# Three taps of q moved to VectorE, the convolutions finished half by half, rank from one difference, and an earlier first low part in a one-core transformer-block kernel

## The reference

```python
x = x + conv_part(_ln_c(x))                     # normalised over the 96 channels
t = tokens(x)                                   # 2304 tokens x 96
t = t + experts(_ln_t(t))
...
# conv_part
qkv = einsum('bchw,oc->bohw', x, w_qkv) + b_qkv
qkv = qkv.reshape(b, 3*c, 24, 2, 24, 2).max(axis=(3, 5))      # 576 pixels are left
qkv = depthwise_conv_3x3(qkv, w_dw) + b_dw                     # nine taps for each channel
q, k, v = split(qkv);  q, k = q/|q|, k/|k|                     # 8 heads of 12 channels
attn = (q @ k.T) * temperature                                 # 12 x 12 in each head
out = sum of topk_softmax(attn, kk) @ v * a_kk   for kk in 6, 8, 9, 9
out = repeat(gelu(out), 2x2) @ w_proj + b_proj
...
# experts: gates from softmax, best 2 of 4, weights renormalised
h = gelu(x @ w1[e] + b1[e]);  y = h @ w2[e] + b2[e];  out = sum of gate[e] * y
```

## Time and profile before

| what | value |
|---|---|
| median of 3 runs | 160.51 us (160.54, 160.51, 158.21) |
| the profiled execution | 157.93 us, of which the span is 156.1 us |
| PE busy | 142.7 us, 91% of the span |
| VectorE (DVE) busy | 116.4 us, 75% |
| ScalarE (ACT) busy | 81.8 us, 52% |
| GpSimd (POOL) busy | 62.3 us, 40% |
| mean granted TensorE clock | 0.952 |

### The profile page before, as it was taken

One profiled execution on the slowest core, in us unless ns is written; L12 is line 12 of the kernel. 1 busy time (PEld: TensorE's weight loads), 2 busy tenths in 40 slices (PEclk: granted clock), 3 DMA queues, 4 the chain that ended last, 5 costly groups with the idle time before them and its releaser, 6 DMA issues.

```text
span 156.1 us, 2515 instructions
## 1 busy us (share of the span) xinstructions
PE 142.7 (91%) x791; PEld 119.8 (77%) x791; DVE 116.4 (75%) x314; ACT 81.8 (52%) x150; POOL 62.3 (40%) x63
## 2 busy tenths in 40 slices
PE   6948968999998897699999999999999999999990
PEld 2423947999988693697866679999999999999950
DVE  0897787999958569956910489998899889899722
ACT  3371768404063243057567763767566566666540
POOL 8999981695000000230050564342332532235250
PEclk9995699999999999569999999999999999999998
DMA  4599100000000000000000001001001001000101
GB/s 142 203 231 264 38 0 4 2 0 0 0 4 0 0 0 2 0 0 4 0 0 0 0 0 42 0 2 38 2 0 38 0 0 35 2 0 4 38 0 38
DMA packets 3750, 4.43 MB, mean 28 GB/s; under 512 B 1934, under 2 KB 3290, under 8 KB 3644
## 3 DMA queue, kind: packets, MB, share of 16 engines
q1 hardware_dynamic: 3338, 3.86, 9.7%
q10 hardware_dynamic: 402, 0.44, 0.8%
HBM read 3.42 MB, written 0.88 MB: 28 GB/s over the span
## 4 chain that ended last, share of the span: by engine, by line
PE 75%; DVE 16%; DMA 3%; ACT 3%; issue 1%; SPq 1%; DVEq 0%
PE psum L937 17%; PE psum L938 16%; PE psum L939 16%; PE psum L1105 8%; PE psum L979 3%; PE psum L975 3%; PE psum L974 3%; DMA xT<-xt 3%; PE psum L1078 3%; DVE stats L665 2%; DVE xn_lo L643 2%; PE psum L932 1%; DVE stats L717 1%; DVE xnT L720 1%; PE psum L910 1%
## 5 line engine op out<-in xcount | busy, mean ns | idle before, releaser
L437 POOL TENSOR_TENSOR xs<-xs,yg 96x384 f32<-96x384 f32 x23 | 26.4, 1147 | 45.4 <-DVE yg L872 37.3
L656 DVE TENSOR_TENSOR h_lo<-hf,h_hi 128x768 fp32r<-128x768 f32 x25 | 34.4, 1375 | 5.2 <-ACT hf L549 4.7
L937 PE MATMUL psum<-xn_hi,w_hi 97*128 97x384 f32 (+1 forms) x72 | 29.7, 413 | 2.2 <-DVE xn_lo L643 2.2
L938 PE MATMUL psum<-xn_hi,w_lo 97*128 97x384 f32 (+1 forms) x72 | 25.4, 353 | 0.0
L939 PE MATMUL psum<-xn_lo,w_hi 97*128 97x384 f32 (+1 forms) x72 | 25.3, 351 | 0.0
L549 ACT ACTIVATE hf<-psum 128x768 f32<-128x768 f32 x25 | 20.2, 809 | 5.7 <-PE psum L939 5.7
L430 POOL TENSOR_TENSOR xs<-xs,pr 96x384 f32<-96x384 f32 x6 | 5.1, 868 | 37.8 <-DVE gs L704 27.8
L937 PEld LDWEIGHTS psum<-xn_hi,w_hi 97*128 97x128 f32 x72 | 14.4, 200 | 5.3 <-issue 4.3
L937 PE MATMUL psum<-h_hi,w_hi 128*96 128x384 f32 x50 | 17.0, 340 | 0.0
L938 PE MATMUL psum<-h_hi,w_lo 128*96 128x384 f32 x50 | 16.8, 336 | 0.0
L939 PE MATMUL psum<-h_lo,w_hi 128*96 128x384 f32 x50 | 16.8, 336 | 0.0
(11 more groups left out here) (173 smaller groups left out, 284.2 us busy)
## 6 DMA issues: line engine op xcount, KB each, us to landing
xs<-x SPq DMA_DIRECT2D x1, 864.0 KB, 10.0
out<-xs SPq DMA_DIRECT2D x6, 144.0 KB, 1.9
w1s<-w SPq DMA_DIRECT2D x1, 576.0 KB
w2s<-w SPq DMA_DIRECT2D x1, 576.0 KB, 6.8
xT<-xt SPq DMA_DIRECT2D x1, 432.0 KB, 5.0
xT<-xt SPq DMA_DIRECT2D x1, 288.0 KB, 3.7
pars<-par ACTq DMA_DIRECT2D x1, 196.5 KB
cst<-consts ACTq DMA_DIRECT2D x1, 170.0 KB, 5.0
```

Of the source, the lines that this page charges most:

```text
L437: pool.tensor_tensor(cols(xs, c), cols(xs, c), cols(yg, e), ALU.add).then_inc(acc_done, 1)
L656: dve.tensor_tensor(lo, h, hi.bitcast(F32), ALU.subtract).then_inc(h_split, 1)
L937: pe.matmul(o, w_hi, m_hi, start=start, stop=False)
L938: pe.matmul(o, w_lo, m_hi, start=False, stop=False)
```

## The change

Four edits, and some that go with them.

1. Taps 0 to 2 of q leave PE. VectorE makes them into a new tile `qpart`, with the bias of q, each one ahead of the same tap of v. q's convolution on PE has taps 3 to 8. VectorE adds PE's half and `qpart` into `qkc`, in place of ScalarE's L508. Tap 8 of v stands beside the first step of k's `rnorm` chain.
2. `conv` does one half of the image to its end (high inputs, then low ones) before the other. ScalarE squares each half of k by itself.
3. The rank is made from `ahead = other - own`, compared with a constant that is 0, or just under 0 for j < i, instead of two comparisons, a product and a sum.
4. `low_from_bank(1, 0)` moves from inside the `rsqrt` of the second norm to ahead of its last two statistics.

With them, ScalarE's high part of `w2` moves ahead of q's diagonals and GpSimd's low part of `w2` ahead of k's; 3 idle products are added behind q's convolution and 2 ahead of the first product.

```diff
-IDLE = {"start": 24, "before scores": 1, "softmax": 1}
+IDLE = {"start": 24, "convolved": 3, "before scores": 1, "softmax": 1, "turned": 2}
...
+Q_TAPS = 3
+KNORM_AT = 8
...
+            pool.wait_ge(w_high, 2)
+            low(w2_lo[:, :], w2s[:, :], w2_hi[:, :], w_split)
             pool.wait_ge(kp_split, 1)
             low(kp_lo[:, :], pooled[:, PAD * PAD:2 * PAD * PAD], kp_hi[:, :], kp_split)
-            pool.wait_ge(w_high, 2)
-            low(w2_lo[:, :], w2s[:, :], w2_hi[:, :], w_split)
...
             for b in range(2):
+                half = slice(PIX + b * HP, PIX + (b + 1) * HP)
                 act.wait_ge(kconv_done, b + 1)
-                act.activation(qkc[:, PIX + b * HP:PIX + (b + 1) * HP], bank(4 + b, cols=HP), ACT.Identity,
+                act.activation(qkc[:, half], bank(4 + b, cols=HP), ACT.Identity,
                                bias=pars[0:C, P_BDW + 1:P_BDW + 2]).then_inc(k_ready, 1)
-            act.wait_ge(k_ready, 2)
-            act.activation(sqj[:, :], qkc[:, PIX:], ACT.Square, accum_out=ssq[:, 1:2]).then_inc(ssq_done, 1)
+                act.wait_ge(k_ready, b + 1)
+                act.activation(sqj[:, b * HP:(b + 1) * HP], qkc[:, half], ACT.Square,
+                               accum_out=ssq[:, 1 + 2 * b:2 + 2 * b]).then_inc(ssq_done, 1)
             act.wait_ge(knorm_done, 1)
             act.activation(khat[:, :], qkc[:, PIX:], ACT.Copy, scale=rnorm[:, 1:2]).then_inc(khat_ready, 1)
-            for b in range(2):
-                act.wait_ge(qmm_done, b + 1)
-                act.activation(qkc[:, b * HP:(b + 1) * HP], bank(b, cols=HP), ACT.Identity,
-                               bias=pars[0:C, P_BDW:P_BDW + 1]).then_inc(qconv_done, 1)
...
                 for k in range(TPC + 7, NT):
+                    if k == NT - 2:
+                        low_from_bank(1, 0)
                     statistics(k)
-                scale(slice(TPC, NT), beside_second).then_inc(ln[1]["rstd"], 1)
+                scale(slice(TPC, NT), None).then_inc(ln[1]["rstd"], 1)
...
+            def whole_tap(g, t, first, o, done):
+                w = pars[0:C, P_DW + 9 * g + t:P_DW + 9 * g + t + 1]
+                if first:
+                    return dve.tensor_scalar(grid(o), tap(g, t), w, pars[0:C, P_BDW + g:P_BDW + g + 1], ALU.mult,
+                                             ALU.add)
+                dve.wait_ge(done, t)
+                return dve.scalar_tensor_tensor(grid(o), tap(g, t), w, grid(o), ALU.mult, ALU.add)
...
+            for t in range(KNORM_AT):
+                if t < Q_TAPS:
+                    whole_tap(0, t, t == 0, qpart[:, :], qtap_done).then_inc(qtap_done, 1)
+                v_tap(t)
...
+            dve.wait_ge(qtap_done, Q_TAPS)
             for b in range(2):
+                dve.wait_ge(qmm_done, b + 1)
+                q = qkc[:, b * HP:(b + 1) * HP]
+                dve.tensor_tensor(q, bank(b, cols=HP), qpart[:, b * HP:(b + 1) * HP],
+                                  ALU.add).then_inc(qconv_done, 1)
                 dve.wait_ge(qconv_done, b + 1)
-                q = qkc[:, b * HP:(b + 1) * HP]
...
-            dve.tensor_tensor(sq3(above), other, own, ALU.is_gt)
-            link(dve.tensor_tensor(sq3(equal), other, own, ALU.is_equal))
-            link(dve.tensor_tensor(equal[:, :], equal[:, :], cst[0:C, K_TRI:K_TRI + DH * DH], ALU.mult))
-            link(dve.tensor_tensor(above[:, :], above[:, :], equal[:, :], ALU.add))
+            link(dve.tensor_tensor(sq3(ahead), other, own, ALU.subtract))
+            link(dve.tensor_tensor(above[:, :], ahead[:, :], cst[0:C, K_TRI:K_TRI + DH * DH], ALU.is_gt))
...
-                pe.wait_ge(split, 2)
-                for b in range(2):
-                    for t in range(9):
+                    pe.wait_ge(split, 2)
+                    for t in taps:
...
-            conv(0, qd_hi, qd_lo, qp_hi, qp_lo, qp_split, qmm_done)
+            conv(0, range(Q_TAPS, 9), qd_hi, qd_lo, qp_hi, qp_lo, qp_split, qmm_done)
```

More of the change, by code:

```diff
@@ L208, in build @@
         sqj = sb("sqj", [C, PIX])
-        ssq = sb("ssq", [C, 3])
+        qpart = sb("qpart", [C, PIX])
+        ssq = sb("ssq", [C, 4])
         n2 = sb("n2", [C, 2])
@@ L220, in build @@
         above = sb("above", [C, DH * DH])
-        equal = sb("equal", [C, DH * DH])
+        ahead = sb("ahead", [C, DH * DH])
         rank = sb("rank", [C, DH])
@@ L396, in _ @@
                 low_diagonal(t)
-            for t in range(9):
+            for t in range(Q_TAPS, 9):
                 w = P_DW + t
@@ L484, in _ @@
             take_high(0, 5)
-            for t in range(9):
+            act.wait_ge(w2_in, 16)
+            act.activation(w2_hi[:, :], w2s[:, :], ACT.Copy).then_inc(w_high, 1)
+            for t in range(Q_TAPS, 9):
                 w = P_DW + t
@@ L681, in beside_first @@
                         statistics(TPC + step - 2)
-                def beside_second(step):
-                    if step == 2:
-                        low_from_bank(1, 0)
                 for k in range(TPC):
@@ L765, in _ @@
             dve.wait_ge(pool_done, V_POOLED)
[L766 to L774, removed]
@@ new lines, in v_tap, with v_beside @@
+            def v_tap(t):
+                whole_tap(2, t, t == 0, vc[:, :], vtap_done).then_inc(vtap_done if t < 8 else v_ready, 1)
+            for t in range(KNORM_AT):
+                if t < Q_TAPS:
+                    whole_tap(0, t, t == 0, qpart[:, :], qtap_done).then_inc(qtap_done, 1)
+                v_tap(t)
+            def v_beside(step):
+                if KNORM_AT + step < 9:
+                    v_tap(KNORM_AT + step)
+            dve.wait_ge(ssq_done, 2)
+            link(dve.tensor_scalar(n2[:, 1:2], ssq[:, 1:2], ssq[:, 3:4], 1e-24, ALU.add, ALU.max), v_beside, 0)
@@ L967, in _, with conv @@
                       cols(xn_lo, c)).then_inc(qkv_done, 1)
-            def conv(at, w_hi, w_lo, p_hi, p_lo, split, done):
+            def conv(at, taps, w_hi, w_lo, p_hi, p_lo, split, done):
                 for b in range(2):
-                    for t in range(9):
+                    for t in taps:
                         d = slice(t * C, (t + 1) * C)
-                        pe.matmul(bank(at + b, cols=HP), w_hi[:, d], tap_of(t, p_hi, b), start=(t == 0), stop=False)
+                        pe.matmul(bank(at + b, cols=HP), w_hi[:, d], tap_of(t, p_hi, b), start=(t == taps[0]),
+                                  stop=False)
                         pe.matmul(bank(at + b, cols=HP), w_lo[:, d], tap_of(t, p_hi, b), start=False, stop=False)
-                pe.wait_ge(split, 2)
-                for b in range(2):
-                    for t in range(9):
+                    pe.wait_ge(split, 2)
+                    for t in taps:
                         ins = pe.matmul(bank(at + b, cols=HP), w_hi[:, t * C:(t + 1) * C], tap_of(t, p_lo, b),
@@ L985, in _ @@
             pe.wait_ge(kp_split, 1)
-            conv(4, diag_hi, diag_lo, kp_hi, kp_lo, kp_split, kconv_done)
+            conv(4, range(9), diag_hi, diag_lo, kp_hi, kp_lo, kp_split, kconv_done)
             pe.wait_ge(pool_done, V_POOLED)
-            pe.wait_ge(qd_set, 18)
+            pe.wait_ge(qd_set, 2 * (9 - Q_TAPS))
             pe.wait_ge(qp_split, 1)
-            conv(0, qd_hi, qd_lo, qp_hi, qp_lo, qp_split, qmm_done)
+            conv(0, range(Q_TAPS, 9), qd_hi, qd_lo, qp_hi, qp_lo, qp_split, qmm_done)
             def turn(g, b):
@@ L998, in turn @@
                 ins.then_inc(qkT_done, 1)
+            idle(IDLE["convolved"], 3)
             pe.wait_ge(khat_ready, 1)
@@ L1056, in turn_gates @@
                 ins.then_inc(gT_done, 1)
+            idle(IDLE["turned"], 0)
             pe.wait_ge(proj_ready, 1)
@@ L1156, in _constants @@
     k[:C, K_CEN:K_CEN + C] = np.eye(C) - 1.0 / C
-    k[:, K_TRI:K_TRI + DH * DH] = np.tril(np.ones((DH, DH)), -1).reshape(-1)
+    k[:, K_TRI:K_TRI + DH * DH] = -np.finfo(np.float32).tiny * np.tril(np.ones((DH, DH)), -1).reshape(-1)
     return k
```

8 lines of the change are left out of this document (2 added, 6 removed).

## The result

| | before | changed |
|---|---|---|
| four runs of each, us | 160.54, 160.51, 158.21, 158.51 | 153.10, 153.08, 151.21, 152.73 |
| median, us | 159.51 | 152.91 |
| ratio of the times, 95% interval | | 0.957 (0.945 to 0.968) |
| later, twelve runs of before and six of changed (`changed_again`), median, us | 156.59 | 152.87 |
| ratio there | | 0.975 (0.969 to 0.981) |

The changed kernel is faster. How much faster depends on the runs that one happens to get of the kernel before: its medians lie between 156.6 and 159.5, and the second ratio leaves open whether the gain is a full 2%.

The account below looks back on a forecast made before the run. Bound: the chain through PE's convolutions, ScalarE's q bias and VectorE's small steps to the attention weights, then chunk 0's low part in the second norm. 157.93 - 2.0 - 3.0 = 152.9, plus 1.4 gives 154.3; range 152.0 to 157.3.

Parts of the forecast that it names:

- Case A: Whole kernel: both gains arrive, 2.0 us up to the attention and 3.0 in the second norm, giving 154.3; chance 0.50.
- The taps: VectorE: from 31.6, six interleaved taps 0.75 us apart and five dependent ones 0.85 apart end at 40.35.
- q's squares: VectorE behind k's chain: alternating additions and squares for q end at 45.05 against 46.60, 1.55 us gained.
- The rank and the attention: VectorE's ranking: two dependent steps of 0.34 us replace 1.23, 0.55 gained; 2.0 us gained up to the attention.
- by a hair: PE between scores and weights: its residual products, free 1.8 us earlier, make it barely later than the weights, 2.1 earlier.
- The second norm: Low part of chunk 0 moved up: first expert product 1.7 us earlier, clock at 1.00, `turn_back(1, 1)` 3.0 us earlier.
- The 1.4 us added for the runs: Whole runs: the mean of before's runs, 159.3, lies 1.4 us above the profiled time, so 1.4 is added.
- rival B: Clock falls in chunk 0 or during the projections, so only the earlier start counts: 3.7 us gained, 155.6; chance 0.25.
- C: VectorE's first taps slow, 1.50 us each, or GpSimd still in their way: total gain 3.5 us, 155.8; chance 0.13.
- D: Second norm: `proj_ready` or `w_split`, not the low part, holds the first product; only 2.0 us left, 157.3; chance 0.02.
- E: Clock falls at PE's waits, 43.6 to 45.5: 5.5 us more, 159.8, chance 0.06; also into the stream, 162, chance 0.04.

Follow-up runs that it names:

- `changed_again`: The changed kernel run once more with no further edit; median 152.87 us, ratio 0.975.
- `no_idles`: The changed kernel without the three idle products behind q's convolution and the two behind the second projection; 152.75 us, ratio 0.974.
- `pool_back`: The changed kernel with GpSimd's and ScalarE's order of before for `w2`; 166.36 against 156.57 us, ratio 1.061.
- `rank_only`: The kernel before with only the rank made from one difference, one run; 154.34 us.
- `fill_gap`: The kernel before with nine idle products in PE's wait ahead of the first expert product, low part not moved; 155.61 against 158.12 us, ratio 0.987.
- `taps4`: The changed kernel with four taps of q on VectorE instead of three; median 151.7 us, ratio without the two long runs 0.971.
- `taps4_idle`: The changed kernel with four taps of q on VectorE and eight idle products behind q's convolution instead of three; median 151.6 us, ratio 0.970.

## Why the prediction was right, point by point

The median of 152.91 lies 1.4 below the forecast of 154.3 and in the range; one of the four runs, 151.21, lies below it. Case A came true in its steps. Without the 1.4 added at the end the forecast would have been 152.9, the median itself, and that is partly luck: the runs lie near 151.3 or near 153.0, and the median goes by how many of each there are.

**The taps.** Expected: first taps of 0.75, a distance of 0.75 between interleaved ones, start after `gateT`'s clear. Measured: 0.85 and 0.75, distances of 0.77 and 0.67, and a start at 31.47 beside that clear. The cost of GpSimd's small steps was put too low: without them the two took 0.58 and 0.57 (`no_idles`). k's `khat` began at 42.76, expected 43.1. `pool_back` shows that the order of GpSimd's work carried this term. The estimate by the Trainium skill, "VectorE: DVE Perf Modes", section "Mode 2×_2P", 0.4 us for each first tap, isn't reached: 0.85 and 0.75 us in the changed profile, and 0.58 and 0.57 in `no_idles`, with 0.49 from one start to the next. No run undoes edit 2, the order by halves, and its worth stays open.

**q's squares.** The term was 1.55 us and measured 2.10 (46.60 to 44.50): the start, the eleven taps, the chain with its tap, and the steps of addition and square each came a tenth or more below what I took. q's first square began at 43.13, expected 43.6. The sum itself has small slips, which change nothing else: 40.35 + 0.85 + 2.0 is 43.2 and not 43.1, four steps of 0.50 are 2.0 and not 1.95, and so the term is 1.4; and 157.93 - 2.6 - 3.0 is 152.3 and not 152.2. Since PE is the later one behind this, the half microsecond more does not reach the time.

**The rank and the attention.** Expected 0.68 us for the ranking, measured 0.67; scores expected at 45.5, measured 45.48; attention 2.0 us earlier, measured 2.08, with taps that began 0.22 later. What was off is "by a hair". VectorE had `att_blk` at 50.27, and PE turned it at 50.82, behind the last residual product and an idle one. Over half a microsecond of VectorE's gain is idle, and `rank_only` shows it: 0.25 of 0.57 arrive.

**The second norm.** Expected 3.0 us, with the first expert product near 60.0, a clock of 1.00 and a wait of 1.3 us. Measured 2.8 (4.85 less 2.08), 59.81, 1.00 and 1.36. What misleads is the split: 1.7 for the earlier start and 1.3 for the clock, less the new wait. It holds only in that order of counting. `fill_gap` counts the other way: the clock alone gives 2.5, and the start adds 0.2, because `xnT` is late next either way. Whoever had read the split as two separate gains would have expected 1.3 of `fill_gap`, and rival B's early start at a low clock, the 1.7, was never run.

**The 1.4 us added for the runs.** This is the term that put the forecast too high. It came from two runs of 160.5 us among the three of before; in the 30 later runs of that kernel none was above 159.1. Those fall into two groups by their mean granted clock: 155.5 to 156.6 us at 0.973 to 0.978, and 158.1 to 159.1 at 0.952 to 0.957. The profiled execution, 157.93 at 0.952, belongs to the second. The changed kernel's ten runs are 151.2 to 151.4 us at 0.989 to 1.000 and 152.7 to 153.2 at 0.977 to 0.989. By their medians the lower groups lie 5.0 us apart (156.3, 151.3) and the upper ones 5.3 (158.3, 153.0), against the 5.0 of the sum. That the groups answer to each other is argued from the clock, not shown; the clocks of the changed kernel's two groups meet at 0.989.

**The rivals.** B, a fall in chunk 0 at the new wait of 1.36 us, did not come in either profile of the changed kernel. C and D didn't come: the first taps took under 0.9 us, and the first product came as early as forecast. E is the one that I priced wrongly. Its place was right, the wait for `khat`; its mechanism is real, as `taps4` and `pool_back` show. But I took 5.5 us for it and 2.1 for the stretch behind, 7.6 together, and the low clock lasted through 24 to 27 us, at a price of 9 us in `taps4` and 10.3 in `pool_back`. In the changed kernel PE has no wait of over 0.5 us there, and none of ten runs met it; that this is the reason fits `taps4_idle` and isn't proved.

## What to carry to other kernels

Read the granted clock behind each wait of the bounding engine: here a wait of 2 us cost 2.5 us more in the products that followed, and filling it with idle products gave nearly as much as removing it. Before a tap or a row is shifted to VectorE, look at what GpSimd does beside its first instructions, and at the slack behind: one tap more brought a loss of 9 us in two of five runs, and GpSimd's old order one of 13 us in all four. After each gain ask what is late next; where the answer is a wait, the cheapest edit may be to pull ready products ahead of it, which gave a further 1.3 us here.

## What was not expected of the hardware

The low clock can outlast its cause by far. In `pool_back` PE was busy for 26.47 of 27.10 us and the clock stayed at its lower level, 1.2 GHz; in `taps4` 23.14 of 23.70. The 36 products of 100 columns in this stretch took 7.89 us there and 4.19 in the changed kernel.

```profile
51.38 7.89 PE L1029 MATMUL psum<-cst,xs 96*128 96x100 f32 x36
```

In both it rose again within 1 us of the start of the first expert product (73.12 and 67.39). In the first norm, at 22 us and in chunk 0 the falls of the other profiles ended after 3.4 to 6.9 us. What makes the difference is open.

The same kernel's falls also come and go from run to run, with an unchanged program: at 12 us, at 22 us or not at all. The spread between its runs goes with it, about 1.8 us for one fall of the changed kernel (153.1 against 151.3).
